# First layer of a four-layer graph network: the update product's h part is made inside the first attention

## What is computed

```
x_norm   = layer_norm(h, g, b)                      # [1250, 768]
out1     = gat_conv(x_norm, W1, ..., heads=4, ch=192)   # attention over edges, [1250, 768]
out2     = gat_conv(out1,   W2, ..., heads=2, ch=96)    # [1250, 192]
x        = x + concatenate([h, out2], -1) @ Wu + bu     # Wu: [960, 768]
```

## Time and profile before

| | |
|---|---|
| median of 3 runs | 4069.36 us (4063.9 to 4070.57) |
| profiled execution, its own time | 4071.57 us |
| its span | 4069.7 us |
| PE busy | 3319.4 us (82%) |
| DVE busy | 1869.0 us (46%) |
| ACT busy | 1090.0 us (27%) |
| POOL busy | 512.4 us (13%) |
| granted TensorE clock, mean | 0.886 of full speed |

### The profile page before, as it was taken

One profiled execution on the slowest core, in us unless ns is written; L12 is line 12 of the kernel. 1 busy time (PEld: TensorE's weight loads), 2 busy tenths in 40 slices (PEclk: granted clock), 3 DMA queues, 4 the chain that ended last, 5 costly groups with the idle time before them and its releaser, 6 DMA issues. The chain is left out here.

```text
span 4069.7 us, 55709 instructions
## 1 busy us (share of the span) xinstructions
PE 3319.4 (82%) x21922; PEld 3173.3 (78%) x21923; DVE 1869.0 (46%) x3441; ACT 1090.0 (27%) x1910; POOL 512.4 (13%) x682
## 2 busy tenths in 40 slices
PE   7925588676898568993879926999999999999898
PEld 7814578576898467883768805999999999999898
DVE  6757686665232587756565573222122221321111
ACT  2303233232343232231322211222332221322212
POOL 0001000010110252100211001102121211210110
PEclk9956798587899689996889957999999999999999
DMA  1221210022112221111110032223232322321312
GB/s 24 53 63 33 32 38 15 13 65 87 41 44 61 80 45 47 42 31 67 39 31 28 20 118 87 61 71 90 82 94 64 84 57 60 89 59 47 104 54 71
DMA packets 279466, 232.87 MB, mean 57 GB/s; under 512 B 108947, under 2 KB 264508, under 8 KB 279175
## 3 DMA queue, kind: packets, MB, share of 16 engines
q1 hardware_dynamic: 166225, 163.33, 14.7%
q10 hardware_dynamic: 112950, 65.63, 5.8%
HBM read 194.98 MB, written 33.94 MB: 56 GB/s over the span
## 5 line engine op out<-in xcount | busy, mean ns | idle before, releaser
L2414 PE MATMUL psum<-p_w_hi,h_lo 128*125 128x384 f32 (+1 forms) x1680 | 533.7, 318 | 48.2 <-POOL p_w_lo L2183 32.5
L2415 PE MATMUL psum<-p_w_lo,h_hi 128*125 128x384 f32 (+1 forms) x1680 | 531.7, 317 | 0.0
L2417 PE MATMUL psum<-p_w_hi,h_hi 128*125 128x384 f32 (+1 forms) x1680 | 530.7, 316 | 0.0
L2475 PE MATMUL psum<-p_c_st,p_v_lo 125*128 125x312 f32 (+1 forms) x1800 | 510.3, 309 | 13.7 <-ACT p_c_st L2242 13.7
L1808 PE MATMUL psum<-v,g_e 125*125 125x193 f32 (+4 forms) x2320 | 428.7, 344 | 102.2 <-DVE g_e L1613 102.0
L2475 PE MATMUL psum<-p_c_st,p_v_hi 125*128 125x312 f32 (+1 forms) x1800 | 508.6, 308 | 0.0
L1808 PEld LDWEIGHTS psum<-v,g_e 125*125 125x125 f32 x2320 | 387.3, 203 | 135.0 <-DVE g_e L1613 56.1
L2242 ACT CAST p_c_st<-p_c 125x624 fp32r<-125x624 uint16 (+2 forms) x450 | 286.0, 679 | 390.2 <-DMA p_c<-c_dram 208.1
L2324 DVE TENSOR_TENSOR p_v_lo<-psum,p_v_hi 125x384 fp32r<-125x384 f32 (+1 forms) x210 | 109.0, 519 | 549.7 <-ACT p_v_hi L2258 549.7
L2414 PEld LDWEIGHTS psum<-p_w_hi,h_lo 128*125 128x125 f32 x1680 | 316.4, 188 | 53.7 <-POOL p_w_lo L2183 30.0
L2475 PEld LDWEIGHTS psum<-p_c_st,p_v_lo 125*128 125x128 f32 x1800 | 337.5, 190 | 15.8 <-ACT p_c_st L2242 15.8
(11 more groups left out here) (253 smaller groups left out, 6237.1 us busy)
## 6 DMA issues: line engine op xcount, KB each, us to landing
p_c<-c_dram ACTq DMA_DIRECT2D x45, 761.7 KB
p_w_raw<-in_L_gnn_w_rel_dram SPq DMA_DIRECT2D x96, 192.0 KB
p_c<-c_dram ACTq DMA_DIRECT2D x30, 610.4 KB
p_c<-c_dram ACTq DMA_DIRECT2D x15, 766.6 KB
p_w_raw<-in_L_gnn_W_dram SPq DMA_DIRECT2D x84, 128.0 KB
c_dram<-counts SPq DMA_DIRECT2D x15, 610.4 KB
res_dram<-g_fin SPq DMA_DIRECT2D x70, 125.0 KB
p_scale<-inv_dram SPq DMA_DIRECT2D x54, 156.0 KB, 3.2
```

What stands on the lines that cost most here:

```text
L2414: pe.matmul(prod, lo[:, b, cols], w_hi[:, slot, :w], start=(b == 0), stop=False)
L2415: pe.matmul(prod, hi[:, b, cols], w_lo[:, slot, :w], start=False, stop=False)
L2417: ins = pe.matmul(prod, hi[:, b, cols], w_hi[:, slot, :w], start=False, stop=end)
L2475: return pe.matmul(ps[:, 2 + u % UB, :n], v[:, b, off:off + size], counts_at[:, :n], start=start, stop=stop, skip_group_check=True)
```

## The change

attention g0 gets `slots=4` (6 before) and a fill: two jobs of 384 columns over the six blocks of h_t with Wu[0:768], adding x in place of a bias, and storing to res_dram. One tile's product follows the sums of steps 2, 4, 6, 8 and 9 of each of the four heads, 20 in all. With a fill, attention uses six PSUM banks for its sums and two for the product (eight for the sums before). split_products p2 keeps only the two blocks of o_t with Wu[768:960], and adds bias and res_dram in place of x. To carry x, the fill loads a 125x384 tile per product (f_x, two places) on SP, for tile f + 2 right after the store of tile f.

```diff
-                        load_w(j + 1, range(RAW if soon else kb))
+                        load_w(j + 1, range(min(RAW, kb) if soon else kb))
...
+            f_x = sb("f_x", [P, 2, fw], F32) if jobs[0].x is not None else None
...
+                def load_x(f):
+                    if f >= n_tiles or jobs[0].x is None:
+                        return
+                    j, t = divmod(f, NT)
+                    if f >= 2:
+                        sp.wait_ge(fin_made, f - 1)
+                    sp.dma_start(f_x[:, f % 2, :jobs[j].w.shape[1]],
+                                 jobs[j].x.rearrange("(t p) f -> p t f", p=P)[:, t]).then_inc(f_x_in[f % 2], 16)
...
                 for s in range(total):
                     for f in at_step[s - 1]:
                         store(f)
+                        load_x(f + 2)
...
+                    if jobs[j].x is not None:
+                        dve.wait_ge(f_x_in[f % 2], 16 * (f // 2 + 1))
...
-                    dve.tensor_tensor(fin[:, f % 2, :w], ps[0:P, 6 + f % 2, :w], f_bias[:, at:at + w],
+                    dve.tensor_tensor(fin[:, f % 2, :w], ps[0:P, 6 + f % 2, :w],
+                                      f_x[:, f % 2, :w] if jobs[j].x is not None else f_bias[:, at:at + w],
                                       ALU.add).then_inc(fin_made, 1)
...
-                        attention(nc, k, "g0", 4, 192, v, k.parts[:, :, 0:4], rows=rows0, given=2)
+                        attention(nc, k, "g0", 4, 192, v, k.parts[:, :, 0:4], rows=rows0, given=2, slots=4,
+                                  fill=([Job(w["L0_Wu"][0:D, c], "acc", x=a["x"][:, c], out=res_dram[:, c])
+                                         for c in chunks(D, 384)], columns(h_t),
+                                        {NT * h + b: 1 for h in range(4) for b in (2, 4, 6, 8, 9)}))
...
-                split_products(nc, k, "p2", columns(h_t) + columns(o_t, 192, 96),
-                               [Job(w["L0_Wu"][:, c], "acc", bias=w["L0_bu"][c], fin="add_x", x=a["x"][:, c],
+                split_products(nc, k, "p2", columns(o_t, 192, 96),
+                               [Job(w["L0_Wu"][D:, c], "acc", bias=w["L0_bu"][c], fin="add_x", x=res_dram[:, c],
                                     out=x_dram[:, c]) for c in chunks(D, 384)])
```

More of the change, by code:

```diff
@@ L1400, in attention @@
         if jobs:
-            f_bias = sb("f_bias", [P, sum(j.w.shape[1] for j in jobs)], F32)
+            f_bias = sb("f_bias", [P, sum(j.w.shape[1] for j in jobs)], F32) if jobs[0].bias is not None else None
             w_raw = sb("w_raw", [128, RAWS, fw], F32)
@@ L1430, in attention @@
         f_bias_in = sem("f_bias_in")
+        f_x_in = [sem(f"f_x_in{n}") for n in range(2)]
         raw_in = [sem(f"raw_in{n}") for n in range(RAWS)]
@@ L1491, in _ @@
                     sp.dma_start(vec[:], bias.partition_broadcast(P)).then_inc(vec_in, 16)
+                for f in range(2):
+                    load_x(f)
                 at = 0
-                for j in jobs:
+                for j in jobs if n_tiles and jobs[0].bias is not None else ():
                     sp.dma_start(f_bias[:, at:at + j.w.shape[1]], j.bias.partition_broadcast(P)).then_inc(f_bias_in, 16)
@@ L1656, in finish @@
                     dve.wait_ge(filled, f + 1)
-                    if f == 0:
+                    if f == 0 and f_bias is not None:
                         dve.wait_ge(f_bias_in, 16 * len(jobs))
+                    if jobs[j].x is not None:
+                        dve.wait_ge(f_x_in[f % 2], 16 * (f // 2 + 1))
                     if f >= 2:
                         dve.wait_ge(stored[f % 2], 16 * (f // 2))
-                    dve.tensor_tensor(fin[:, f % 2, :w], ps[0:P, 6 + f % 2, :w], f_bias[:, at:at + w],
+                    dve.tensor_tensor(fin[:, f % 2, :w], ps[0:P, 6 + f % 2, :w],
+                                      f_x[:, f % 2, :w] if jobs[j].x is not None else f_bias[:, at:at + w],
                                       ALU.add).then_inc(fin_made, 1)
```

## The result

The changed kernel takes 4154.5 us (median of four runs, 4144.1 to 4157.0), the kernel before 4068.9 us on the same chip: a ratio of 1.021 with a 95% interval of 1.019 to 1.023, 85.7 us slower. The forecast was 4135 us, 4106 to 4155. The profiled execution of the changed kernel is the fastest of the four (4144.05 us, span 4142.3, mean clock 0.878). The stages behind the changed ones, whose code is the same, take 3084.0 us in it and 3094.3 us in the profile of before; in the profiles of the experiments that share this code they take 3084.7 to 3101.6 us, so these 10 us are not the change's.

A forecast was written before the change was run, and what follows sets the result against it. In g0 PE and DVE were both taken as nearly full, and p2 as bound by PE. The terms +85 (g0) and -19 (p2) gave +66 us on the median of 4069.36, so 4135 us, range 4106 to 4155.

The forecast's parts named there:

- g0: First attention: DVE's wait in finish delays the next scores and weights, so the fill costs +85 us (75 to 93).
- p2: Update product: PE keeps 6 of 24 matmuls per tile, the x loop paces tiles at 3.85 us: -19 us (-12 to -32).
- The forecast's own case: Whole kernel: +85 in g0 and -19 in p2, range +45 to +81, 4114 to 4150 us, chance 0.68.
- rival 2: g0: read_rest queues behind store and x load, each 4 us late, 3 x 4 = +12, so 4147 us; chance 0.12.
- Rival 4: p2: at 4.36 us a tile it saves only 10 us, so +75, 4144 us; chance 0.10.
- head 0: First head of g0: first product ends near 516.6, three pairs bring 551.4, sums of step 9 end at 554.7.
- heads 1 and 2: Middle heads of g0, with `largest` steps: 68.8 us each against 48.2 before.
- head 3: Last head of g0, without `largest`: 57.4 us.
- The tail: Behind g0's last sums: last product, finish and store add +4 us (3.7 to 4.7).
- The pair: Steps 4 to 9 of g0's heads: two steps with one product take 5.0 + 0.1 + 3.3 + 3.2 = 11.6 us.
- rival 3: p2's x loop freed of its queue: DVE's 1.7 us a tile saves 58 to 60 us; alone +25, 4094 us.
- Rival 1: g0: finish holds nobody, PE absorbs the fill, last sums +39.5; whole +21, 4090 us; chance 0.07.

The follow-up runs named there:

- the run for the second six: Changed kernel with GpSimd's splitting of the second job's six weight blocks cut to 8 columns, that job multiplying by the first's blocks: 4145.4 against 4070.0 us.
- the kernel that arranges for this: Changed kernel with row vectors first on SP, products behind steps 1, 3, 5, 7, 9, and finish, split_low, store and x load one step later: 4118.9 us.
- the pair of runs with all transfers cut: Row transfers in 120 and 5 partitions: kernel before 3997.5 us; change with later finish, steps 1, 3, 5, 7, 9, row vectors first 4015.7; both against 4070.0.
- the run with the early row vector: Changed kernel with head 0's write_rest at step 1 and read_rest at step 2 for 4 and 5: 4158.7 against 4067.1 us.

## Why the prediction was right, and where its terms were off

The sign and the mechanism of both parts held, and p2 its size. The size of g0 did not: its end moved by +101.2 us (start of t1) for +85, outside the part's own 75 to 93, and the sum was 20 us short (+66 for +85.7). The forecast's own case reached to 4150; 4154.5 lies inside 4106 to 4155 only because the range had been widened for rivals 2 and 4, and neither came about at its price. That the range holds is in part luck. The 16 us that g0 is over the forecast are, from the first scores on: 5.6 to head 0's first product, 2.4 in its pairs, 7.8 in heads 1 and 2, 0.3 in head 3 and 0.6 at the start, less 0.5 at the tail.

- **The pair.** 11.6 us forecast, 11.44 measured; product to weights 5.0 and 4.8; idle of PE before the second sums 1 to 2 and 1.49. That DVE's wait couples the engines was shown by moving it: 34.7 us.
- **Head 0** should have had its first product's end 22.2 us behind the first scores (516.6 - 494.43); it came 27.8 us behind them (519.9 - 492.04). Five of these 5.6 us are DVE's own: from the first scores to the end of weights(2) the same instructions take 15.0 us before (494.43 to 509.40) and 20.1 after (492.04 to 512.16), with no wait in either. The difference is that GpSimd splits six blocks there; scores take 2.25 us for 1.52. That these six are the cause rests on these rows and on the run for the second six; it was not tried by itself. Another 2.9 is the pair that ends with the product of step 8, 14.33 us (539.44 to 553.77) for 11.44: 1.10 us of waiting for read_rest, then PE idle 2.69 and sums of 5.21 us at a granted clock of 0.67. That is rival 2, "a row vector comes late", with its cover of 1 us, once and not three times: +3 for +12. Its cause, the scattered writes at the start, was not in the rival. (The reciprocal at 561.85 stands 1.65 us behind the last sums, which end at 560.2, since DVE comes to it late.)
- **Heads 1 and 2**: +2.1 and +5.7. This is the term that was mis-sized: the prediction calls POOL's splitting "beside all this [...], unless it slows DVE: up to 3 us, kept for the range", and puts it at nothing in the sum. Without the second six blocks both heads take 68.2, so GpSimd costs 7.7 to 9.1 us in these two heads alone, and with the five of head 0 some 13 to 14 (an estimate from these rows) of the 16 us that were missing in g0.
- **Head 3**, which has neither `largest` nor GpSimd beside it: from the product of step 8 of head 2 to the last sums 61.0 us (702.5 to 763.5) for 60.7. The tail: 771.71 - 763.52 = 8.2 us to the next stage, 4.7 before, +3.5 for the forecast +4. The gain at the start was 2.4 for 3.
- **Six banks and slots=4**: the slots cost nothing by their own run. The banks were not tried by themselves, but the chain with them comes to 68.2 for 68.8.
- **p2**: -19.8 for -19 (its own sum, 952 for 970.43, gives -18.4), first `p_fin` 8.5 us behind the first load (980.73 - 972.28) for 8.4, tiles at 3.68 to 3.95 us for 3.85, clock at 0.52, share at 0.32. What kept rival 3 off is the rule of the Trainium skill (DMA: Bandwidth & Descriptors, section "Why a DMA increments its semaphore by 16 and not by 1") that a transfer uses the largest number of engines, at most 16, that divides its outer sizes: five for 125 rows, fifteen for 120. The runs agree: 120 + 5 rows gave nearly the rival's time, 56.2 us for p2, and took the change from +85.7 to +56.3, by 29 us.
- **The rivals.** Rival 1 (PE absorbs the fill, 4090) needed DVE not to wait; the kernel that arranges for this came to 4119. Its last reciprocal stands at 728.5, 62.6 us behind before's and not 39.5 (the prediction's own terms add up to 707.3 and not "near 705", so 41.5), as PE still waits in heads 1 to 3 for weights (11.6 us) and for w_lo (5.6), and 5.1 in head 0. Rivals 1 and 3 together, foreseen at 4049 and so below before, would come to +46.5 - 29.4 = +17 us by these two runs, an estimate; the pair of runs with all transfers cut, +18.2, bears it out. Rival 4 did not occur.

The lesson is in the term and not in the total: a slowdown that had been seen as possible was bounded by a guess and then left out of the sum, and 4154.5 came to lie at the very end of the range.

## What to carry to other kernels

Matmuls that fill another engine's gap cost what their post-processing holds up. Look where the wait for their result stands in an in-order queue: finishing one step later made the same 360 matmuls 35 us cheaper, and back to back they made g0's heads 14 to 20 us shorter than spread out. Count the splitting on GpSimd as VectorE's time where VectorE is near the path. And a loop at a DMA share near 5/16 on transfers of 125 rows is not free of its DMAs: cutting all row transfers into 120 and 5 rows was worth 72 us on the kernel before, while the change itself paid in no form that was tried.

## What was not expected of the hardware

- 120 + 5 rows for 125 raised the rate in p2 from 101 to 153 GB/s and the DMA share from 0.32 to 0.56 (170 and 0.61 in steady tiles); one more issue of about 0.34 us on SP per move did no harm.
- GpSimd and VectorE slow each other: 1.52 us became up to 2.25 on VectorE, 0.51 became 1.73 on GpSimd; a small VectorE instruction (125x10, two inputs) took 0.83 us for 0.17 there (502.97 in the changed kernel, 503.21 before). An eight-column cast on GpSimd waited for VectorE (1.09 us for 0.19), whose `largest` kept its 1.46.
- A scattered write of a row vector held SP's issue for 9.7 us, and SP's next transfer left at 524.96, 20 us after the first of two such writes (504.60 in the run with the early row vector).
- The clock in the changed kernel: behind 1.49 us of idle PE the sums took 3.53 us at a granted clock of 1.00 (from 524.77), behind 2.69 us 5.21 at 0.67 (from 548.86), behind 8.94 us 5.75 at 0.60 (from 575.87); the last two are means between the two levels.
